# GpSimd splits each attention weight block in four pieces of 256 columns

## The chip, the cores and the metric

The kernel runs as one program on one core of a Trainium2 chip. The time is the device time of one execution in microseconds (us). Engine names in the rows: PE is TensorE (PEld its weight loads), DVE is VectorE, ACT is ScalarE, POOL is GpSimd, SP issues the DMAs of this kernel's weights.

## The reference

Two post-norm decoder layers over 1024 tokens (16 sequences of 64) of width 512, in fp32. Only the two grouped attentions matter here: layer 0's cross-attention (called B in the kernel, with rotary tables) and layer 1's self-attention (called D, with a sliding window). Each has 32 query heads and 8 key heads of 128:

```python
# B: _L0_xattn_ref (D is the same without cos/sin, with its own mask)
q = (query @ Wq).reshape(nb, q_len, H, D).transpose(0, 2, 1, 3)
k = (key @ Wk)...; v = (value @ Wv)...
q = q * cos + _rotate_half(q) * sin
k = k * cos + _rotate_half(k) * sin
scores = jnp.einsum('bhqd,bhkd->bhqk', q, k) / jnp.sqrt(jnp.float32(D))
attn = jax.nn.softmax(scores, axis=-1)
x = jnp.einsum('bhqk,bhkd->bhqd', attn, v)
return x @ Wo
...
x = _layernorm(x + _L0_xattn_ref(x, ctx_4096, ...), axis=-1)
```

## The kernel before

fp32 products are made of reduced-precision ones. Each operand is held as a high part (the value rounded to fp32r) and a low part (what is left), and a product is three matmuls: high by high, high by low, low by high (`three`). So each weight must be split before TensorE can use it. GpSimd does this in `grouped_attention`: a block of 128 partitions by 1024 columns (`BLK`) arrives by DMA in one of two buffers `raw`; `high_part` (L78) adds zero to it and writes the high part as fp32r; after a wait on `w_high`, L694 subtracts the high part from the raw block and writes the low part, which raises `w_low`.

An attention runs over 4 pairs of key heads. `START` projects values, keys and the first queries; then three loop passes (`TURN`, in a hardware loop) and one last pass (`LAST`) follow. A pass has 16 units u (`SLOTS`): two key heads (u = 0 to 7 and 8 to 15) by 8 token tiles. GpSimd splits 4 blocks in `START` (v, k, q0, q1), 10 per loop pass (o0, o1, q0, q1, k, v, o2, o3, q2, q3) and 6 in `LAST`: 40 blocks per attention, 80 in both. The o blocks are the output weights `wo`, the q blocks the query weights `wq`. A block's split may begin when TensorE has stopped using the old contents: o0 and o2 wait for `wo_used` (the first half of the last output product of a head), o1 and o3 for `y_done` of that tile, q0 to q3 for the query projection that used them last. GpSimd takes the blocks strictly in that order.

What TensorE does in the units that matter, in its own order:

- u = 7 or 15: output product of the head's last tile (L83, bankY from `wo` and `oT`), in whose middle `wo_used` is raised.
- u = 0 or 8: transposes of the softmax (L791, wait for `prob`, DVE's L950), scores of a later unit (L764), probabilities by values (L803), a query projection (L83, bankA from `xT` and `wq`).
- u = 1 or 9: transposes, scores, L803, then output(u - 1), which waits for o1 or o3 (`w_low`), then a query projection.
- u = 2 or 10: transposes, output(u - 1), L803, then scores of unit u + 2, which in B wait for the rotated queries of the last projection (`qk_done`, DVE's L925), then further projections.

DVE does per unit L932 (mask, reads PSUM), L936 (maximum), L939 (subtract), L944 (sum), L947 (reciprocal), L950 (multiply), L978 (low part of the head's output, reads PSUM) and L955 (residual, reads PSUM). In B it also rotates the queries: L919 (reads PSUM), L921 and L925. L939, L950, L921 and L925 are `tensor_tensor` with both inputs in SBUF.

The lines that the change touches:

```python
high_part(dst[name][0], raw[n % 2][:]).then_inc(w_high, 1)
pool.wait_ge(w_high, part.weights + n + 1)
nc.gpsimd.tensor_tensor(dst[name][1], raw[n % 2][:], f32(dst[name][0]), ALU.subtract).then_inc(w_low, 1)
```

Of the kernel before, what the change touches and what calls it, by code (L numbers as in the profile page):

```python
# [11 lines left out]
ALU = mybir.AluOpType  # L12
# [21 lines left out]
BLK = 1024  # L34
# [4 lines left out]
def f32(ap):  # L39
    return ap.bitcast(F32)  # L40


def build_program(nc, io):
# [3 lines left out]
    def sb(stack, name, shape, dt=F32):  # L47
        return stack.enter_context(nc.sbuf_tensor("sb_" + name, shape, dt))

    def sem(name):  # L50
        return ctx.enter_context(nc.semaphore(name))
# [6 lines left out]
    raw = [sb(ctx, f"raw{i}", [P, BLK]) for i in range(NRAW)]  # L58
# [17 lines left out]
    def high_part(dst, src):  # L76

        return nc.gpsimd.tensor_tensor(dst, src, zero[0:src.shape[0]].to_broadcast([src.shape[0], src.shape[1]]), ALU.add)  # L78
# [126 lines left out]
    w_high = sem("A_whigh"); w_low = sem("A_wlow"); zeroed = sem("A_zeroed")  # L205
# [361 lines left out]
    only_qk = lambda order: [x for x in order if x[0] in "QK"]  # L567
    TURN_BANKS, TURN_QK = len(TURN), len(only_qk(TURN))

    START_BLOCKS = ["v", "k", "q0", "q1"]  # L570
    TURN_BLOCKS = ["o0", "o1", "q0", "q1", "k", "v", "o2", "o3", "q2", "q3"]
    LAST_BLOCKS = ["o0", "o1", "q0", "q1", "o2", "o3"]

    class Part:

        def __init__(self, it, order, blocks):
# [3 lines left out]
            if started:  # L580
                self.banks, self.qks, self.weights = self.banks + len(START), self.qks + len(only_qk(START)), self.weights + len(START_BLOCKS)

# [21 lines left out]

    assert not any(len(x) % 2 for x in (START, TURN, LAST, START_BLOCKS, TURN_BLOCKS, LAST_BLOCKS))
    group_names = ("w_high", "w_low", "padded", "a_ready", "swapped", "roped", "turned", "qk_done", "v_done",
# [4 lines left out]
    def grouped_attention(tag, norm, first, source, rope, following):  # L611
# [6 lines left out]
        with ExitStack() as mem:  # L618
# [25 lines left out]
            dst = {"k": [w[:].rearrange("p h k n -> p (h k n)") for w in wk], "v": [w[:].rearrange("p k n -> p (k n)") for w in wv]}  # L644
# [4 lines left out]
            def run(engine, start, turn):  # L649

                start(Part(first, START, START_BLOCKS))
                with engine.Fori(first, final) as it:
                    turn(Part(it, TURN, TURN_BLOCKS))
                turn(Part(final, LAST, LAST_BLOCKS))

            with nc.Block() as block:
                @block.sync
                def _(sp):
                    if rope:
                        sp.dma_start(mask[:], io["mask"]).then_inc(in_bound, 16)  # L660
                    else:
                        sp.dma_start(bound[:], io["causal"]).then_inc(in_bound, 16)

                    def load(part):
                        for n in range(len(part.blocks)):
                            at = part.weights + n
                            if part.order is START and n < NRAW:
                                continue
                            sp.wait_ge(w_low, at - 1)
                            src = io["w_attn"][at] if part.order is not TURN else io["w_attn"][bass.ds(at, 1)].rearrange("a p c -> p (a c)")  # L670
                            sp.dma_start(raw[n % 2][:], src).then_inc(w_raw[n % 2], 16)
                    run(sp, load, load)
                    load_ahead(sp, w_low, (first + NPAIR) * len(TURN_BLOCKS), *following)

                @block.gpsimd
                def _(pool):
                    def split(part):
                        for n, name in enumerate(part.blocks):
                            if part.order is not START:
                                if name == "o0":  # L680
                                    pool.wait_ge(wo_used, part.it * 2 + 1)
                                elif name == "o1":
                                    pool.wait_ge(y_done, part.it * SLOTS + 2)
                                elif name == "o2":
                                    pool.wait_ge(wo_used, part.it * 2 + 2)
                                elif name == "o3":
                                    pool.wait_ge(y_done, part.it * SLOTS + NT + 2)
                                else:
                                    used = {"q0": ("Q", 5), "q1": ("Q", 7), "k": ("Q", 5), "v": ("Q", 5), "q2": ("Q", 13), "q3": ("Q", 15)}[name]
                                    pool.wait_ge(a_ready, part.bank(used) + 1)  # L690
                            pool.wait_ge(w_raw[n % 2], (part.weights + n - n % 2) * 8 + 16)
                            high_part(dst[name][0], raw[n % 2][:]).then_inc(w_high, 1)
                            pool.wait_ge(w_high, part.weights + n + 1)
                            nc.gpsimd.tensor_tensor(dst[name][1], raw[n % 2][:], f32(dst[name][0]), ALU.subtract).then_inc(w_low, 1)  # L694
                            if part.order is START and name == "k":
                                nc.gpsimd.memset(kt[:], 0.0).then_inc(padded, 1)
                    run(pool, split, split)
# [835 lines left out]
```

## Time and profile before

| | us |
|---|---|
| three runs | 1838.74, 1838.44, 1837.08 |
| median | 1838.44 |
| span of the profiled execution | 1832.8 |
| median less that span | 5.6 |
| PE busy | 1679.7 |
| DVE busy | 1065.0 |
| ACT busy | 603.0 |
| POOL busy | 525.5 |
| DMA of one raw block, from issue to landing (median of 80) | 3.5 |

The profiled execution's own time is its span of 1832.8 us from the first to the last instruction and what lies around it, for which 5.6 us is taken, the distance to the median. Attention B lies at about 260 to 938 us of the span, D at about 991 to 1583 us. In the timeline rows below an instruction has its start, its duration, its engine, line and operation, what it writes and reads, a count, and in brackets how long its engine had stood idle and who ended that. An instruction's duration includes time in which it was already issued and could not proceed.

### The profile page before, as it was taken

What the parts mean: (1) busy time and instruction counts of PE and PEld (TensorE: products, weight loads), DVE (VectorE), ACT (ScalarE), POOL (GpSimd) and SP (SyncE); (2) the same over time, 40 slices, a digit from 0 to 9 for tenths busy, and PEclk for the clock granted to TensorE, in tenths of its full rate; (3) what the DMA queues carried; (4) which work ended last, traced back from release to release, by engine and by line L of the source; (5) the groups of instructions that cost most, each with busy time, mean ns of one, the idle gap of its engine ahead of it and who ended that gap; (6) DMA issues with size and microseconds to landing.
All of it is one profiled execution on the core that took longest, in us unless ns stands there. A gap on an engine that the chain in (4) does not pass through costs nothing. (4 is left out here: it accounts for less than half of the span.)

```text
span 1832.8 us, 24019 instructions
## 1 busy us (share of the span) xinstructions
PE 1679.7 (92%) x8910; PEld 1336.7 (73%) x8910; DVE 1065.0 (58%) x2105; ACT 603.0 (33%) x1199; POOL 525.5 (29%) x297
## 2 busy tenths in 40 slices
PE   8897879889998988989888999999999999888998
PEld 6665658667776866777677777777877877676866
DVE  3878775766676577566754245355265245517645
ACT  2564533223322323232243222222222222425541
POOL 4316123330323052120133323233053031432330
PEclk9998999899998989999999999999999999999999
DMA  4002011110111020000010111011021010112231
GB/s 178 14 18 81 25 35 46 47 35 12 36 35 46 1 70 24 23 24 24 23 42 27 57 35 47 12 57 46 0 69 46 0 46 24 47 33 61 71 91 46
DMA packets 26173, 75.78 MB, mean 41 GB/s; under 512 B 3904, under 2 KB 4640, under 8 KB 25824
## 3 DMA queue, kind: packets, MB, share of 16 engines
q1 hardware_dynamic: 25696, 73.42, 12.4%
q8 instruction: 66, 1.08, 0.2%
q0 software_dynamic: 384, 1.05, 0.2%
q14 instruction: 27, 0.22, 0.0%
HBM read 72.36 MB, written 2.10 MB: 41 GB/s over the span
## 5 line engine op out<-in xcount | busy, mean ns | idle before, releaser
L83 PE MATMUL bankA<-sb_xT,sb_Bwq 128*128 128x512 f32 x768 | 196.7, 407 | 0.0
L83 PE MATMUL bankY<-sb_Bwo,sb_BoT 128*128 128x512 f32 x768 | 195.9, 405 | 0.2 <-DVE sb_BoT L978 0.2
L83 PE MATMUL bankY<-sb_Dwo,sb_DoT 128*128 128x512 f32 x768 | 192.3, 399 | 2.0 <-POOL sb_Dwo L694 1.8
L83 PE MATMUL bankA<-sb_xT,sb_Dwq 128*128 128x512 f32 x768 | 189.9, 396 | 0.0
L83 PEld LDWEIGHTS bankY<-sb_Bwo,sb_BoT 128*128 128x128 f32 x768 | 142.8, 192 | 44.2 <-issue 15.0
L83 PEld LDWEIGHTS bankA<-sb_xT,sb_Bwq 128*128 128x128 f32 x768 | 147.4, 195 | 36.0 <-issue 2.7
L83 PEld LDWEIGHTS bankY<-sb_Dwo,sb_DoT 128*128 128x128 f32 x768 | 139.8, 188 | 44.0 <-issue 10.9
L83 PEld LDWEIGHTS bankA<-sb_xT,sb_Dwq 128*128 128x128 f32 x768 | 142.3, 188 | 33.9 <-issue 2.7
L919 DVE TENSOR_TENSOR sb_BqT<-bankA,sb_Btable 128x512 f32<-128x512 f32 x64 | 44.3, 692 | 183.5 <-ACT sb_Bsw L842 183.5
L78 POOL TENSOR_TENSOR sb_Bwo<-sb_raw,sb_zero 128x1024 fp32r<-128x1024 f32 x16 | 31.3, 1955 | 372.9 <-PE bankY L83 364.3
L78 POOL TENSOR_TENSOR sb_Dwo<-sb_raw,sb_zero 128x1024 fp32r<-128x1024 f32 x16 | 31.6, 1973 | 335.1 <-PE bankY L83 335.1
L932 DVE TENSOR_TENSOR sb_Dsc<-bankA,sb_Dbound 128x256 f32<-128x256 f32 x64 | 27.0, 422 | 158.6 <-PE bankA L764 158.6
L955 DVE TENSOR_TENSOR sb_xtok<-sb_xtok,bankY 128x512 f32<-128x512 f32 x128 | 87.1, 680 | 51.8 <-PE bankY L83 51.7
L842 ACT ACTIVATE sb_Bsw<-bankA 64x512 f32<-64x512 f32 x160 | 94.8, 593 | 54.8 <-PE bankA L83 51.7
L978 DVE TENSOR_TENSOR sb_DoT<-bankO,sb_DoT 128x512 fp32r<-128x512 f32 x64 | 43.7, 683 | 109.4 <-ACT sb_DoT L880 109.4
L764 PE MATMUL bankA<-sb_Bkt,sb_BqT 128*128 128x128 f32 x512 | 77.8, 300 | 27.7 <-DVE sb_BqT L925 24.1
L764 PEld LDWEIGHTS bankA<-sb_Bkt,sb_BqT 128*128 128x128 f32 x512 | 69.7, 211 | 34.5 <-DVE sb_BqT L925 23.3
L921 DVE TENSOR_TENSOR sb_Bsw<-sb_Bsw,sb_Btable 128x512 f32<-128x512 f32 x80 | 85.3, 1066 | 0.0
L874 ACT ACTIVATE sb_Dpt<-bankT 128x256 f32<-128x256 f32 x64 | 24.6, 384 | 184.4 <-PE bankT L791 184.4
L336 PE MATMUL bankA<-sb_Akt,sb_Aqm 128*128 128x128 f32 x512 | 71.9, 286 | 5.8 <-ACT sb_Aqm L416 4.2
L874 ACT ACTIVATE sb_Bpt<-bankT 128x256 f32<-128x256 f32 x64 | 24.6, 384 | 157.6 <-PE bankT L791 157.5
L854 ACT ACTIVATE sb_Bsc<-sb_Bsc 128x256 f32<-128x256 f32 x64 | 26.6, 416 | 138.8 <-DVE sb_Bsc L939 138.8
(253 smaller groups left out, 3406.3 us busy)
## 6 DMA issues: line engine op xcount, KB each, us to landing
sb_raw<-in_w_attn SPq DMA_DIRECT2D x80, 512.0 KB, 3.5
sb_raw<-in_q_gu SPq DMA_DIRECT2D x22, 256.0 KB, 2.7
sb_raw<-in_q_d SPq DMA_DIRECT2D x11, 256.0 KB, 2.6
sb_rawx<-in_xT SPq DMA_DIRECT2D x4, 512.0 KB, 8.0
sb_raw<-in_wqk SPq DMA_DIRECT2D x8, 256.0 KB, 2.6
sb_xtok<-in_x_tok SPq DMA_DIRECT2D x1, 2048.0 KB, 12.7
sb_raw<-in_ctxT SPq DMA_DIRECT2D x4, 512.0 KB, 3.8
sb_raw<-in_ctx_tok SPq DMA_DIRECT2D x4, 512.0 KB, 3.8
```

The source lines that it names most:

```text
L78: return nc.gpsimd.tensor_tensor(dst, src, zero[0:src.shape[0]].to_broadcast([src.shape[0], src.shape[1]]), ALU.add)
L83: last = nc.tensor.matmul(out, lhs, rhs, start=start and i == 0, stop=stop and i == len(pairs) - 1)
L336: done = nc.tensor.matmul(bankA[n % 2][:, j * P:(j + 1) * P], qm[quad % 2][:, j, 2 * m:2 * m + 2, :].rearrange("p e q -> p (e q)"), window ...
L764: done = nc.tensor.matmul(bank[:, at:at + P], qT[:, 2 * t + b, 2 * hp:2 * hp + 2, :].rearrange("p h q -> p (h q)"), window(kt, 2 * t + b, ...
L842: nc.scalar.activation(sw[part.swap(x)][64 * i:64 * i + 64, :], bankA[part.buffer(x)][64 - 64 * i:P - 64 * i, :], ACT.Copy).then_inc(swapp ...
L854: nc.scalar.activation(flat, flat, ACT.Exp, scale=HD ** -0.5).then_inc(st["exp"], 1)
L874: nc.scalar.activation(pt[u % 2][:], bankT[u % 2][:, 0:GROUP * S], ACT.Copy).then_inc(pt_done, 1)
L919: nc.vector.tensor_tensor(to, bankA[part.buffer(x)][:].rearrange("p (b s) -> p b s", s=S), table[:, 0, half].rearrange("p (b s) -> p b s", ...
L921: nc.vector.tensor_tensor(b[:], b[:], table[:, 1, half], ALU.mult).then_inc(turned, 1)
L932: nc.vector.tensor_tensor(s3, bankA[part.buffer(("S", u))][:].rearrange("p (a c) -> p a c", a=2)[:, :, S:S + P], bound_of(u).unsqueeze(1). ...
L955: nc.vector.tensor_tensor(xtok[:, t, :], xtok[:, t, :], bankY[u % 2][:], ALU.add).then_inc(y_done, 1)
L978: nc.vector.tensor_tensor(oT[u % 2][1][:].rearrange("p h b q -> p b h q"), bankO[:, :, 0:GROUP * S].rearrange("p b (h q) -> p b h q", h=GR ...
```

## The change

Each block is split in four pieces of 256 columns: the high part of a piece, a wait for it, its low part, then the next piece. `w_high` now counts pieces; `w_low` still counts blocks and is raised by the low part of the last piece. All 80 blocks of the two grouped attentions are cut; the splits of the other stages are not.

```diff
+    PIECES = 4
...
-                            high_part(dst[name][0], raw[n % 2][:]).then_inc(w_high, 1)
-                            pool.wait_ge(w_high, part.weights + n + 1)
-                            nc.gpsimd.tensor_tensor(dst[name][1], raw[n % 2][:], f32(dst[name][0]), ALU.subtract).then_inc(w_low, 1)
+                            for i in range(PIECES):
+                                piece = slice(i * BLK // PIECES, (i + 1) * BLK // PIECES)
+                                high_part(dst[name][0][:, piece], raw[n % 2][:, piece]).then_inc(w_high, 1)
+                                pool.wait_ge(w_high, (part.weights + n) * PIECES + i + 1)
+                                low = nc.gpsimd.tensor_tensor(dst[name][1][:, piece], raw[n % 2][:, piece], f32(dst[name][0][:, piece]), ALU.subtract)
+                                if i == PIECES - 1:
+                                    low.then_inc(w_low, 1)
```

GpSimd's queue at the head of the loop body of attention B, before, with the semaphores that each row waits for (blocks o0 and o1; D's loop is the same with sb_Dwo; the register operations compute the values of the waits):

```order
L691 ISA [waits G_wo_used]
L78 TENSOR_TENSOR sb_Bwo0<-sb_raw0,sb_zero 128x1024 [waits G_raw0]
L693 REGISTER_ALU
L694 TENSOR_TENSOR sb_Bwo1<-sb_raw0,sb_Bwo0 128x1024 [waits G_w_high]
L683 ISA
L78 TENSOR_TENSOR sb_Bwo0<-sb_raw1,sb_zero 128x1024 [waits G_raw1,G_y_done]
L693 REGISTER_ALU
L694 TENSOR_TENSOR sb_Bwo1<-sb_raw1,sb_Bwo0 128x1024 [waits G_w_high]
```

The same place in the changed kernel, up to the end of block o0 and the first piece of o1:

```order
L78 TENSOR_TENSOR sb_Bwo0<-sb_raw0,sb_zero 128x256
L696 REGISTER_ALU
L697 TENSOR_TENSOR sb_Bwo1<-sb_raw0,sb_Bwo0 128x256 [waits G_w_high]
L78 TENSOR_TENSOR sb_Bwo0<-sb_raw0,sb_zero 128x256
L696 REGISTER_ALU
L697 TENSOR_TENSOR sb_Bwo1<-sb_raw0,sb_Bwo0 128x256 [waits G_w_high]
L684 ISA
L78 TENSOR_TENSOR sb_Bwo0<-sb_raw1,sb_zero 128x256 [waits G_raw1,G_y_done]
L696 ISA
L697 TENSOR_TENSOR sb_Bwo1<-sb_raw1,sb_Bwo0 128x256 [waits G_w_high]
```

No instruction moved against another: a pair of instructions became four pairs, a low part is followed by the next high part with no wait between them inside a block, and the queues of the other engines are the same.

## Rows read from the trace of the kernel before

**Rows 1.** The page: the span, and each engine's busy time
```profile
span 1832.8 us, 24019 instructions
PE 1679.7 (92%) x8910; PEld 1336.7 (73%) x8910; DVE 1065.0 (58%) x2105; ACT 603.0 (33%) x1199; POOL 525.5 (29%) x297
```

**Rows 2.** PE's waits: who waited for whom, us in total, times, longest
```profile
PE bankT L791 <- DVE sb_Bsc L950: 28.0, 9, 4.7
PE bankA L764 <- DVE sb_BqT L925: 24.1, 13, 3.7
...
PE bankT L791 <- DVE sb_Dsc L950: 6.0, 8, 0.8
...
PE bankY L83 <- POOL sb_Dwo L694: 1.8, 7, 0.3
```

**Rows 3.** POOL's groups of instructions: 256-column splits elsewhere, busy us, mean ns
```profile
L1004 POOL TENSOR_TENSOR sb_Fagu<-sb_raw,sb_Fagu 128x256 fp32r<-128x256 f32 x1 | 0.7, 724 | 0.1
L78 POOL TENSOR_TENSOR sb_Fagu<-sb_raw,sb_zero 128x256 fp32r<-128x256 f32 x1 | 0.6, 613 | 46.1 <-POOLq L1161 46.1
```

**Rows 4.** Timeline of attention D, a head's change, POOL, DVE and PE
```profile
1097.76 1.89 POOL L78 TENSOR_TENSOR sb_Dwo<-sb_raw,sb_zero 128x1024 fp32r<-128x1024 f32 x1 [33.31 <-PE bankY L83]
...
1100.63 3.04 PE L83 MATMUL bankA<-sb_xT,sb_Dwq 128*128 128x512 f32 x12
...
1102.08 2.07 POOL L78 TENSOR_TENSOR sb_Dwo<-sb_raw,sb_zero 128x1024 fp32r<-128x1024 f32 x1
...
1102.32 2.11 DVE L950 TENSOR_TENSOR sb_Dsc<-sb_Dsc,sb_Dri 128x256 f32<-128x256 f32 x1
...
1104.23 2.42 POOL L694 TENSOR_TENSOR sb_Dwo<-sb_raw,sb_Dwo 128x1024 fp32r<-128x1024 f32 x1
...
1104.49 0.44 PE L791 MATMUL bankT<-sb_ident,sb_Dsc 128*128 128x128 f32 x2 [0.81 <-DVE sb_Dsc L950]
...
1106.70 3.03 PE L83 MATMUL bankY<-sb_Dwo,sb_DoT 128*128 128x512 f32 x12 [0.25 <-POOL sb_Dwo L694]
```

**Rows 5.** Timeline of attention B, a head's change, POOL, DVE and PE
```profile
391.70 1.89 POOL L78 TENSOR_TENSOR sb_Bwo<-sb_raw,sb_zero 128x1024 fp32r<-128x1024 f32 x1 [39.30 <-PE bankY L83]
392.11 2.03 DVE L921 TENSOR_TENSOR sb_Bsw<-sb_Bsw,sb_Btable 128x512 f32<-128x512 f32 x1
...
393.67 2.71 POOL L694 TENSOR_TENSOR sb_Bwo<-sb_raw,sb_Bwo 128x1024 fp32r<-128x1024 f32 x1
...
394.24 2.69 DVE L925 TENSOR_TENSOR sb_BqT<-sb_BqT,sb_Bsw 128x512 f32<-128x512 f32 x1
...
394.58 3.04 PE L83 MATMUL bankA<-sb_xT,sb_Bwq 128*128 128x512 f32 x12
...
399.71 2.56 DVE L950 TENSOR_TENSOR sb_Bsc<-sb_Bsc,sb_Bri 128x256 f32<-128x256 f32 x1
...
402.32 0.69 PE L791 MATMUL bankT<-sb_ident,sb_Bsc 128*128 128x128 f32 x2 [4.70 <-DVE sb_Bsc L950]
...
405.61 3.01 PE L83 MATMUL bankY<-sb_Bwo,sb_BoT 128*128 128x512 f32 x12
```

**Rows 6.** Timeline of attention B, units 2 and 10: rotated queries and scores
```profile
413.93 2.45 DVE L921 TENSOR_TENSOR sb_Bsw<-sb_Bsw,sb_Btable 128x512 f32<-128x512 f32 x1
...
417.36 1.16 PE L764 MATMUL bankA<-sb_Bkt,sb_BqT 128*128 128x128 f32 x8 [2.34 <-DVE sb_BqT L925]
...
508.34 2.08 PE L764 MATMUL bankA<-sb_Bkt,sb_BqT 128*128 128x128 f32 x8 [3.60 <-DVE sb_BqT L925]
```

**Rows 7.** PE behind another wait, and stretches of B and D: busy us, then granted clock
```profile
890.51 0.69 PE L791 MATMUL bankT<-sb_ident,sb_Bsc 128*128 128x128 f32 x2 [4.61 <-DVE sb_Bsc L950]
...
894.00 4.34 PE L83 MATMUL bankY<-sb_Bwo,sb_BoT 128*128 128x512 f32 x12
...
294.00:938.00 644.00, 581.25 (x2897) 462.98 (x2896) 438.51 (x775) 197.78 (x375) 151.04 (x68) 0.95 0.09 29
991.00:1583.00 592.00, 578.56 (x3040) 465.35 (x3040) 268.48 (x543) 152.43 (x308) 175.48 (x81) 1.00 0.11 36
```

## The prediction

> **What bounds the kernel now.** I read the page first: TensorE is busy for 92% of the span and GpSimd for 29% [rows 1], so GpSimd's own time counts only where TensorE waits for it, directly or through VectorE. The view of TensorE's waits shows both. In B it waits 28.0 us for L950 and 24.1 us for L925; in D only 6.0 us for L950, and 1.8 us for GpSimd's low parts of wo, 7 times [rows 2]. Then the timelines show why. In B, L921, L925, L939 and L950, which read both inputs from SBUF, take 2.03, 2.69 and 2.56 us where 0.68 and 0.42 us are their undisturbed times; they end 0.3 to 0.55 us after the GpSimd instruction that ran when they were issued: L950, issued at 399.71, ends at 402.27 [rows 5]. So a 2 us GpSimd instruction holds VectorE, and TensorE stands for 4.70 us behind it. GpSimd is held in turn, but for less: the L694 behind L921 takes 2.71 us instead of 2.40, the L78 behind L939 in D 2.07 us instead of 1.89 [rows 4, 5].
>
> In D the second limit is visible. GpSimd begins o0 at 1097.76, ends o1 at 1106.65, and the output product starts at 1106.70 having waited 0.25 us for it [rows 4]. There is no slack there, at 7 places.
>
> **What a block costs.** A high and a low part of 256 columns exist elsewhere: 613 and 724 ns [rows 3]. With the 0.08 us between a high part and its low part (1097.76 + 1.89 to the next start) and the 0.03 us by which the next high part overlaps, a piece is 0.61 + 0.08 + 0.73 - 0.03 = 1.39 us, a block 5.56 us. Now it is 1.89 + 0.08 + 2.40 - 0.03 = 4.34 us. Each of 80 blocks grows by 1.22 us, 98 us of GpSimd time. 0.1 us either way per piece is my bound on this. For all blocks but o0 to o3 that growth is hidden: q, k and v blocks are used several units later, and the v block of D's start, needed soonest, ends just where TensorE finishes its transposes (0 to 0.1 us if that cover is gone). A DMA of a raw block waits for the block before last and lands in some 3.5 us, less than the 5.56 us of the block between.
>
> **D: seven heads' changes (slower).** New o0 and o1: 2 x 5.56 = 11.1 us, and four collisions with L939 and L950, at 0.04 to 0.18 us (the 2.07 against 1.89 is the largest [rows 4]), 0.4 us: GpSimd ends at 1097.76 + 11.6 = 1109.35. TensorE no longer waits 0.81 us for L950 and stands ready at about 1105.5, so it waits 3.9 us, and the output product starts 1109.40 - 1106.70 = 2.70 us later. 7 x 2.70 = 18.9 us. Nothing gives that back: VectorE and ScalarE wait for TensorE here.
>
> The Trainium skill (SBUF — State Buffer, Who interferes with whom) says that the loser of the port that GpSimd and VectorE share "fully blocks" for the whole instruction. Whole durations of 0.42 us for each of the four VectorE instructions would make the collisions 1.7 us and the sum 1.3 us more at each of the seven places; the rows show at most 0.18 us, so this case's trace does not bear out that price for GpSimd.
>
> **The clock.** D has a granted clock of 1.00 over its whole stretch, which is 2.4 GHz; B has 0.95, so about a tenth of B's time is at 1.2 GHz [rows 7]. In B each of the eight waits of 3.6 us or more is followed by such a time. Its price: from the transposes to the end of the output product, D needs 4.99 us without its wait [rows 4], B after its long waits 6.30 us at the least (402.32 to 408.62 [rows 5]) and 7.83 at the most (890.51 to 898.34 [rows 7]). The five places have a mean of 7.0, so 2.0 us each, bounds 1.3 and 2.8. D's new waits are of that length, so I take 7 x 2.0 = 14.0 us. Below stands 0: no D wait of before is long enough to show it. D's short wait of 0.48 us for L950 near its start goes: -0.4. D: 18.9 + 14.0 - 0.4 = +32.5 us.
>
> **B: heads' changes (about nothing).** Five of the seven look like rows 5, with waits of 4.6 to 4.7 us. With pieces, L921 and L925 each wait for at most one piece; L950 then ends at about 397.0, before TensorE ends its projection at 397.62. The 4.70 us are gone. What is late next is o1. GpSimd needs 11.1 us and meets eight colliding instructions, four of 512 columns at 0.31 to 0.45 us and four of 256 at 0.04 to 0.18: 1.9 us. It ends at 391.70 + 13.0 = 404.7, where the output product started at 405.61: 0.8 us earlier. TensorE stands 5.4 us ahead of it, so the 2.0 us of the slow clock now lie behind the start, where 0.6 us of them lay before (the product takes 3.01 to 4.34 us [rows 5, 7], mean 3.6, against 3.03). Net -0.8 + 2.0 - 0.6 = +0.6, five times +3 us. The other two changes, behind the loop's branch, had their output product 12.5 us after GpSimd's start; the same steps give 12.3: 0.
>
> **B: scores after the rotation (faster).** At 413.93 L921 waits for a whole high and low part (2.45 us), and the scores wait 2.34 us for L925 [rows 6]. GpSimd starts q1 at the end of the same projection, 2.43 us before L921 is issued. With pieces L921 ends 1.0 us after its issue (the piece that runs, then 0.55), L925, issued 0.3 us later, 0.7 us after that, and the scores start 1.4 us earlier than at 417.36, four places, -5.6. At three places L925 is held by the k block too (3.6 to 3.7 us [rows 6]); these end at the same 0.9 us: 3 x 2.75 = -8.3. One wait of the same kind at B's first units, within the 28.0 us of [rows 2], -1.7. The slow clock behind the three long ones (scores take 2.08 us instead of 1.16 [rows 6]) goes at 2.0 us each, behind two of the others at 1.5: -9.0, bounds 3 and 12. Sum -24.6, with the heads' changes -21.6 us.
>
> **Sum.** +32.5 - 21.6 = +10.9 us. On the profiled execution: span 1832.8 to 1843.7, and with the 5.6 us around it 1849.3, against the median of 1838.4. About 0.2%, 3.7 us, is what a measurement of this kernel can tell from no change.
>
> **Rivals.**
> *The clock stays high in D* (or VectorE's head start hides it). For it: D has lost no clock so far, its GpSimd waits were short. Against: B's long waits, all eight. 10.9 - 14.0 = -3: 1835 us.
> *Pieces cost less than their single rows*, because dispatch overlaps in a row of them; at 1.25 us a piece, o0 and o1 take 10.0 + 0.5 us: D +1.6 and +1.5 clock each, 22; B's five heads' changes 1.1 us earlier each, -2.5 in all; -24.6 stays, and the shorter waits save some 8 of clock in B. About -13: 1825 us. Against: the 0.03 us overlap is all that the rows show.
> *GpSimd is held for whole VectorE instructions*, which decides if VectorE wins every boundary: at D 1.3 us more each (9), at B's five 2 us (10), 20 in all: 1869 us. Against: the 2.07 and 2.71 us.
> *The change does not do what it says*: inside a block no wait separates a low part from the next high part, so VectorE might not get in there. Then B keeps its waits and GpSimd only grows: +32 in D, +5 in B: 1875 us. Against: the L78 of 1102.08 was issued before its predecessor's end and still yielded 0.18 us [rows 4].
>
> **How the numbers follow.** Forecast 0.60, its own range 1841 to 1858 (clock terms 1.3 to 2.8, pieces 0.05 either way); clock stays high 0.15; cheaper pieces 0.12; GpSimd held 0.08; no effect on VectorE 0.05. The range 1830 to 1866 leaves out the cheap pieces and half of the last two. Slower: 0.55 of the forecast and 0.13, 0.68. Same: 0.05 of the forecast and 0.10 of the clock case, 0.15. Faster: 0.12 and 0.05, 0.17.
>
> **What would show it.** L939, L950, L921 and L925 at most near 1.3 us; the 28.0 us for L950 in B nearly gone, L925 near 9 us; waits of PE for the low part of wo of about 3.9 us seven times in D and 5 us five times in B; D's granted clock down to about 0.97, B's near 0.96. Wrong if D's waits for GpSimd are under 2 us, if D's clock stays at 1.00, or if VectorE's instructions still take 2 us.

## The result, and the profile after

| | before | after |
|---|---|---|
| median, us | 1837.81 (1837.08 to 1838.74, 4 runs) | 1850.76 (1849.32 to 1854.07, 4 runs) |
| span of the profiled execution | 1832.8 | 1847.5 |
| attention B, from its first transposes to C's | 676.7 | 652.6 |
| attention D, the same way | 592.4 | 627.9 |
| all the rest of the span | 563.7 | 567.0 |
| POOL busy | 525.5 | 629.4 |
| DVE busy | 1065.0 | 965.4 |

The changed kernel is slower by 0.7%: ratio 1.007, 95% interval 1.0056 to 1.0084. A fourth run of before moved its median from the 1838.44 of the prediction to 1837.81. The forecast of 1849.3 us is 1.5 us below the measured median, the direction is right, and both attentions moved as forecast: B gained 24 us (forecast 21.6), D lost 35.5 us (forecast 32.5).

In the changed kernel the lines that concern us have moved: L694 is L697, L764 is L769, L791 is L796, L921 is L926, L925 is L930, L939 is L944 and L950 is L955. The page of after, which answers to [rows 1]:

```profile
span 1847.5 us, 24679 instructions
PE 1684.7 (91%) x8910; PEld 1342.2 (73%) x8910; DVE 965.4 (52%) x2105; ACT 602.3 (33%) x1199; POOL 629.4 (34%) x777
```

GpSimd has 480 instructions more and is busy 104 us longer; VectorE has the same 2105 instructions and is busy 100 us less, because it no longer stands issued behind GpSimd. TensorE's waits (total us, times, longest), which answer to [rows 2]:

```profile
PE bankY L83 <- POOL sb_Dwo L697: 29.7, 7, 4.4
PE bankY L83 <- POOL sb_Bwo L697: 28.2, 7, 5.7
...
PE bankA L769 <- DVE sb_BqT L930: 10.0, 13, 1.0
...
PE bankT L796 <- DVE sb_Bsc L955: 1.5, 2, 1.1
```

The wait for L955 in B fell from 28.0 to 1.5 us, the one for the rotated queries from 24.1 to 10.0 us. In their place stand waits for GpSimd itself: 28.2 us in B, where there were none in the list, and 29.7 us in D, where there were 1.8. One more wait fell, which neither the rows nor the prediction name: at B's start TensorE waits for VectorE to copy out the rotary tables. The wait in before and in after, then the two mask instructions that VectorE had to finish ahead of the copies in before, and the first of them in after:

```profile
PE bankO L710 <- DVE sb_Btable L907: 7.6, 1, 7.6
PE bankO L715 <- DVE sb_Btable L912: 3.5, 1, 3.5
```
```profile
268.86 3.86 DVE L903 TENSOR_SCALAR sb_Bhidden<-sb_Bmask 128x1024 f32<-128x1024 int32 x1
...
272.64 2.37 DVE L904 TENSOR_SCALAR sb_Bbound<-sb_Bmask 128x1024 f32<-128x1024 int32 x1
```
```profile
271.28 0.85 DVE L908 TENSOR_SCALAR sb_Bhidden<-sb_Bmask 128x1024 f32<-128x1024 int32 x1
```

So it is not only the `tensor_tensor` instructions with two inputs in SBUF that GpSimd's whole blocks held: these read one. The wait is 4.1 us shorter, a sixth of B's gain. Three of the seven groups of rotation and softmax instructions that GpSimd holds, each with its least, middle and greatest duration in ns (the greatest of the other four are 0.93 to 1.23 us):

```profile
L955 DVE TENSOR_TENSOR sb_Bsc<-sb_Bsc,sb_Bri x64: 416/420/969, 319.5 to 899.7; 128x256 f32<-128x256 f32 x64
L955 DVE TENSOR_TENSOR sb_Dsc<-sb_Dsc,sb_Dri x64: 416/424/968, 1016.8 to 1581.0; 128x256 f32<-128x256 f32 x64
L930 DVE TENSOR_TENSOR sb_BqT<-sb_BqT,sb_Bsw x64: 676/682/1255, 305.1 to 881.4; 128x512 f32<-128x512 f32 x64
```

None is above 1.3 us any more; in [rows 4, 5] they took 2.03 to 2.69. This is what the change does, and what each half of it costs is seen at a head's change. D, on POOL, DVE and PE, from the same timeline view as [rows 4]:

```profile
1079.65 1.02 POOL L697 TENSOR_TENSOR sb_Dwo<-sb_raw,sb_Dwo 128x256 fp32r<-128x256 f32 x1
...
1080.00 0.96 DVE L955 TENSOR_TENSOR sb_Dsc<-sb_Dsc,sb_Dri 128x256 f32<-128x256 f32 x1
...
1081.95 0.38 PE L796 MATMUL bankT<-sb_ident,sb_Dsc 128*128 128x128 f32 x2
...
1087.24 0.95 POOL L697 TENSOR_TENSOR sb_Dwo<-sb_raw,sb_Dwo 128x256 fp32r<-128x256 f32 x1
...
1088.25 5.23 PE L83 MATMUL bankY<-sb_Dwo,sb_DoT 128*128 128x512 f32 x12 [4.39 <-POOL sb_Dwo L697]
```

GpSimd began o0 at 1076.21. VectorE's L955 now takes 0.96 us, the transposes wait for nothing, and TensorE then stands 4.39 us before the output product, because the last low part of o1 ends at 1088.19. From GpSimd's start to the product are 12.04 us; in [rows 4] it was 8.94. And the product behind the wait takes 5.23 us instead of 3.03. B, the same view as [rows 5]:

```profile
383.41 1.05 POOL L697 TENSOR_TENSOR sb_Bwo<-sb_raw,sb_Bwo 128x256 fp32r<-128x256 f32 x1
...
387.07 0.96 DVE L955 TENSOR_TENSOR sb_Bsc<-sb_Bsc,sb_Bri 128x256 f32<-128x256 f32 x1
388.16 0.38 PE L796 MATMUL bankT<-sb_ident,sb_Bsc 128*128 128x128 f32 x2
...
394.91 0.79 POOL L697 TENSOR_TENSOR sb_Bwo<-sb_raw,sb_Bwo 128x256 fp32r<-128x256 f32 x1
395.76 5.04 PE L83 MATMUL bankY<-sb_Bwo,sb_BoT 128*128 128x512 f32 x12 [5.69 <-POOL sb_Bwo L697]
...
408.11 1.16 PE L769 MATMUL bankA<-sb_Bkt,sb_BqT 128*128 128x128 f32 x8 [0.91 <-DVE sb_BqT L930]
```

Here the 4.70 us wait of [rows 5] is gone from the transposes and a wait of 5.69 us stands before the product. The scores of unit 2 (last row) wait 0.91 us where they waited 2.34 [rows 6]. The stretches of B and D (busy us of PE, PEld, DVE, ACT and POOL with their instructions, then the granted clock, the DMA share and GB/s):

```profile
264.20:916.80 652.60, 597.18 (x3056) 478.89 (x3056) 395.10 (x794) 205.00 (x388) 241.27 (x321) 0.96 0.11 34
970.40:1598.30 627.90, 592.03 (x3041) 476.54 (x3042) 231.17 (x543) 152.44 (x308) 218.10 (x322) 0.96 0.11 34
```

D's granted clock went from 1.00 [rows 7] to 0.96, which is time at 1.2 GHz that D had hardly any of before; B's rose from 0.95 to 0.96.

### The profile page after: what moved, and what is told of

The parts are those of the page before. It is cut to its first block and busy times, and to the rows that moved or that the text cites. A ratio compares the mean times of both kernels' runs of the same rounds, so it can differ in the third digit from the quotient of the medians.

```text
span 1847.5 us, 24679 instructions
## 1 busy us (share of the span) xinstructions
PE 1684.7 (91%) x8910; PEld 1342.2 (73%) x8910; DVE 965.4 (52%) x2105; ACT 602.3 (33%) x1199; POOL 629.4 (34%) x777
## 5 line engine op out<-in xcount | busy, mean ns | idle before, releaser
L83 PE MATMUL bankY<-sb_Dwo,sb_DoT 128*128 128x512 f32 x768 | 207.4, 422 | 30.0 <-POOL sb_Dwo L697 29.7
L83 PE MATMUL bankY<-sb_Bwo,sb_BoT 128*128 128x512 f32 x768 | 203.7, 417 | 28.4 <-POOL sb_Bwo L697 28.2
L83 PEld LDWEIGHTS bankY<-sb_Dwo,sb_DoT 128*128 128x128 f32 x768 | 150.6, 202 | 75.8 <-POOL sb_Dwo L697 32.5
L83 PEld LDWEIGHTS bankY<-sb_Bwo,sb_BoT 128*128 128x128 f32 x768 | 148.5, 199 | 73.2 <-POOL sb_Bwo L697 31.0
L78 POOL TENSOR_TENSOR sb_Bwo<-sb_raw,sb_zero 128x256 fp32r<-128x256 f32 x64 | 46.2, 722 | 317.5 <-PE bankY L83 317.5
L78 POOL TENSOR_TENSOR sb_Dwo<-sb_raw,sb_zero 128x256 fp32r<-128x256 f32 x64 | 41.7, 651 | 319.7 <-PE bankY L83 319.7
L769 PE MATMUL bankA<-sb_Bkt,sb_BqT 128*128 128x128 f32 x512 | 69.8, 279 | 14.6 <-DVE sb_BqT L930 10.0
L769 PEld LDWEIGHTS bankA<-sb_Bkt,sb_BqT 128*128 128x128 f32 x512 | 62.2, 191 | 21.4 <-DVE sb_BqT L930 10.6
L336 PEld LDWEIGHTS bankA<-sb_Akt,sb_Aqm 128*128 128x128 f32 x512 | 64.4, 198 | 8.7 <-ACT sb_Aqm L416 6.4
L769 PE MATMUL bankA<-sb_Dkt,sb_DqT 128*128 128x128 f32 x512 | 69.0, 278 | 0.0
```

What stands on the lines that cost most here:

```text
L83: last = nc.tensor.matmul(out, lhs, rhs, start=start and i == 0, stop=stop and i == len(pairs) - 1)
L336: done = nc.tensor.matmul(bankA[n % 2][:, j * P:(j + 1) * P], qm[quad % 2][:, j, 2 * m:2 * m + 2, :].rearrange("p e q -> p (e q)"), window ...
L769: done = nc.tensor.matmul(bank[:, at:at + P], qT[:, 2 * t + b, 2 * hp:2 * hp + 2, :].rearrange("p h q -> p (h q)"), window(kt, 2 * t + b, ...
```

## The experiments

**The theory.** Cutting a block does two separate things. VectorE is held by GpSimd for one piece instead of a whole block, which shortens TensorE's waits for VectorE. And each block takes GpSimd 1.2 us longer, which delays what waits for the whole block: the output product behind o0 and o1, or o2 and o3. The first pays in B, at the scores; the second costs in D, and costs once more because TensorE runs at 1.2 GHz behind the new waits. **The rivals:** the pieces themselves (their interleaving with VectorE, their waits) cause D's loss, not their length; the heads' changes of B carry the gain; VectorE gets in only because of the waits between a high part and its low part.

All versions compute the whole reference. In the diffs `many` is the number of pieces of a block and takes the place of `PIECES`; the values of the waits on `w_high` (`highs_before`, the pieces split so far) follow it. In the kernels of the experiments the lines are numbered again: L711, L713 and L715 are the low part (L694 before), L783 the scores, L810, L812 and L814 the transposes, L944 to L948 the last step of the rotation, L969 to L973 L950.

| kernel | median, us | ratio to before | B, us | D, us | rest |
|---|---|---|---|---|---|
| before | 1839.1 | | 676.7 | 592.4 | 563.7 |
| after | 1850.76 | 1.007 | 652.6 | 627.9 | 567.0 |
| e1: four pieces in B alone | 1819.43 | 0.9897 | 653.6 | 593.6 | 567.2 |
| e2: four pieces in D alone | 1876.03 | 1.0198 | 677.7 | 629.3 | 568.0 |
| e3: q, k, v in four, o whole | 1815.90 | 0.9874 | 653.4 | 593.4 | 567.7 |
| e4: two pieces | 1817.44 | 0.9891 | 640.1 | 604.7 | 567.7 |
| e5: whole blocks, D's o0 and o2 one high part longer | 1861.46 | 1.0127 | 676.8 | 615.4 | 566.3 |
| e6: four pieces, wait in mid-product | 1826.90 | 0.9942 | 641.9 | 616.2 | 566.5 |
| e7: four highs, then four lows | 1839.44 | 1.0007 | 656.3 | 621.2 | 568.5 |
| e8: two pieces in B, wait in mid-product | 1792.73 | 0.9745 | 632.8 | 591.4 | 567.9 |
| e9: B q, k, v in four, o in two; D whole; wait in mid-product | 1782.34 | 0.9690 | 623.6 | 590.5 | 568.8 |

B, D and rest are of each kernel's one profiled execution. The median of before is of the runs beside the first four kernels (1837.8 to 1839.2 beside the others); 0.001 of a ratio is 1.8 us.

### Four pieces in one attention alone

```diff
-                            for i in range(PIECES):
+                            many = 4 if tag == 'B' else 1    # e2: 4 if tag == 'D' else 1
+                            for i in range(many):
```

> Pieces of 256 columns in attention B alone, whole blocks in D. Theory (B gains because VectorE is let in between pieces, D loses because o0 and o1 take GpSimd 3 us longer): B's stage 24 us shorter as in the changed kernel, D's as before, 592 us and clock 1.00; median about 1814. Rival (the loss is not D's own, for instance the clock of the whole program): D's stage is longer than 596 us here too, median over 1820.

> Pieces in attention D alone, whole blocks in B. Theory: B's stage as before (677 us), D's stage 628 us as in the changed kernel, median about 1873. Rival (D's loss was partly brought in from B): D's stage under 615 us, median under 1860.

Measured 1819.43 (ratio 0.9897, 0.988 to 0.9913) and 1876.03 (1.0198, 1.0181 to 1.0215). TensorE's waits with pieces in B alone, then in D alone:

```profile
PE bankY L83 <- POOL sb_Bwo L711: 27.5, 7, 5.4
...
PE bankA L783 <- DVE sb_BqT L944: 10.3, 13, 1.1
...
PE bankT L810 <- DVE sb_Dsc L969: 6.1, 8, 0.8
...
PE bankY L83 <- POOL sb_Dwo L711: 1.8, 7, 0.3
```
```profile
PE bankT L810 <- DVE sb_Bsc L969: 27.2, 9, 4.7
...
PE bankY L83 <- POOL sb_Dwo L711: 30.2, 7, 4.4
```

Each half carries its own rows and leaves the other attention with its rows of before. By stage lengths the halves are -23.1 us in B and +36.9 us in D, 13.8 us together where the whole change has 11.4; by medians -19.7 and +36.9, 17.2 against 13.0. So they add, to within 4 us. The change is a gain of about 20 us and a loss of about 37 us, and no coupling shows beyond those 4 us.

### Where in B the gain is

```diff
+                            many = 1 if name[0] == 'o' else 4
```

> Pieces for the blocks of q, k and v in both attentions; the eight o blocks of each pass whole. Theory: D as before (no q, k or v block is waited for), the 4.7 us waits of B's transposes stay, the seven waits of B's scores for the rotated queries fall from 2.3 to 3.7 us to 0.9 us, and with the clock behind them this is 20 to 25 us: median about 1815. Rival (B's gain came with the waits of the transposes, and the waits of the scores move elsewhere): within 5 us of the kernel before, about 1835.

Measured 1815.90 (0.9874, 0.9857 to 0.989). TensorE's waits:

```profile
PE bankT L810 <- DVE sb_Bsc L969: 26.7, 9, 4.7
PE bankA L783 <- DVE sb_BqT L944: 10.3, 13, 1.0
```

The long waits at B's heads' changes have stayed, because the o blocks are whole, and B is as short as with all blocks cut: 653.4 us against 653.6. The whole gain of B comes with the q, k and v blocks, and cutting o0 to o3 there exchanges 26.7 us of waits for VectorE against 27.5 us of waits for GpSimd (e1). The rival that B's heads' changes carry the gain falls. Most of the gain is at the scores, but not all: the wait for the rotary tables is down to 3.6 us here too. The kernel was profiled once more, to see how well stage lengths repeat (its label says b_only, it is the kernel of e3):

> The version with only the q, k and v blocks in pieces, looked at once more for what its stages take in a second profiled execution: theory: B's stage within 2 us of 653 us, D's within 2 us of 593 us; rival (the stages' times depend on where the slow clock happens to fall by more than that): 5 us or more apart.

One run of 1813.78 us, B 652.1 and D 593.3 against 653.4 and 593.4. The stage lengths of this kernel repeat within 1.4 us, and B's whole blocks take 676.7, 677.7 and 676.8 us in before, e2 and e5, so differences between stages from some 3 us on can be read.

### Two pieces instead of four

```diff
+                            many = 2
```

> Two pieces of 512 columns for all blocks. Theory, from the rows of 512 columns (1.04 and 1.29 us): a block takes 4.76 us; the output product in D starts 1.0 us later seven times, behind waits of 2.2 us, and half of these are followed by a slow clock, +14 us; in B the output products start 2.6 us earlier before clock (-6 us after it) and the scores gain a little less, -21 us: median about 1825. Rival (what costs in D is the mere number of instructions that VectorE can hold, not the length of the two blocks): D's loss is half of the changed kernel's, +17 us, and B as there: 1831.

Measured 1817.44 (0.9891, 0.987 to 0.9911), 7.6 us less than expected. TensorE's waits:

```profile
PE bankA L783 <- DVE sb_BqT L944: 18.1, 13, 2.3
PE bankY L83 <- POOL sb_Dwo L711: 14.8, 7, 2.4
PE bankY L83 <- POOL sb_Bwo L711: 7.8, 6, 1.5
```

D behaves as expected: from GpSimd's start to the product 9.94 us in the mean, 1.0 more than before, and D is 12.3 us longer (14 expected). B gained 36.6 us and not 27. Against e1 its waits for GpSimd are 19.7 us less (7.8, none above 1.5), those at the scores 7.8 us more, those for L969 5.0 us more and the one for the rotary tables 1.1 us more: 5.8 us less in all. B is 13.5 us shorter, so some 7.7 us more lie elsewhere; the slow clock behind the long waits can carry them, for B's granted clock is 0.98 here and 0.96 in e1, and all seven output products behind a head's change take 3.01 to 3.06 us, where five took 5.03 to 5.49 us. This is what I had left out. Where all blocks are cut alike, two pieces are better than four: the smallest piece is not the best.

### Is it GpSimd's length, or the pieces?

Whole blocks everywhere, and in D the high part of o0 and of o2 is written twice, which changes no value and makes GpSimd 2 us later.

```diff
+                            many = 1
+                            if tag == "D" and name in ("o0", "o2"):
+                                high_part(dst[name][0], raw[n % 2][:]).then_inc(w_high, 1)
+                                pool.wait_ge(w_high, highs_before(tag, part, n) + 1)
```

> Whole blocks everywhere as in the kernel before; in D alone the high part of o0 and of o2 is written twice, which adds 1.9 us to GpSimd and no pieces. Theory (D loses what o0 and o1 take longer, plus the clock behind the wait): the output product starts 1.9 us later seven times behind waits of about 2.1 us, the clock costs 0.7 us each: D's stage 592 + 18 = 610 us, median about 1857. Rival (D's loss comes from the pieces themselves, the many instructions and their collisions): D's stage within 3 us of 592, median under 1842.

Measured 1861.46 (1.0127, 1.011 to 1.0144). TensorE's waits and one product behind them:

```profile
PE bankY L83 <- POOL sb_Dwo L715: 15.4, 7, 2.2
```
```profile
1111.07 4.51 PE L83 MATMUL bankY<-sb_Dwo,sb_DoT 128*128 128x512 f32 x12 [2.21 <-POOL sb_Dwo L715]
```

No block is cut, and D is 23.0 us longer: the product starts 1.97 us later at seven places, 13.8 us, and the other 9 us are products and projections at the slow clock, as in the row, 4.51 us instead of 3.03; five of the seven products are like it, two take 3.02 and 3.03. This is the loss of D without the pieces. The rival that pieces as such cause it falls, and the absence of slack that the prediction read from one row, 0.25 us of wait at the product [rows 4], is confirmed: each us on GpSimd there is a us of D, and the slow clock behind the new waits comes on top. That clock cost more than expected here, 1.3 us a place and not 0.7.

### Giving TensorE something to do in the wait

Output product of a head's first tile: the products with the first two heads of the group need only o0 (or o2), those with the last two o1 (or o3). The wait for the second block can stand between them.

```diff
                         if u % NT == 0:
-                            pe.wait_ge(w_low, part.block("o3" if u else "o1"))
+                            pe.wait_ge(w_low, part.block("o2" if u else "o0"))
...
+                        elif u % NT == 0:
+                            product(bankY[u % 2][:], pairs[:len(pairs) // 2], stop=False)
+                            pe.wait_ge(w_low, part.block("o3" if u else "o1"))
+                            product(bankY[u % 2][:], pairs[len(pairs) // 2:], start=False).then_inc(y_ready, 1)
```

> The changed kernel, and TensorE waits for block o0 (or o2) before the output product of a head's first tile and for o1 (or o3) only in the middle of that product, since its first six matmuls use o0 alone. Theory (the low part of o1 ends last): its second half still starts with the end of o1, so six matmuls, 1.45 us and up to 2.4 us at the slow clock, leave the path twelve times, D 10 to 17 us and B 7 to 12 us shorter: median about 1830. Rival (the wait is for what stands before o1, or the clock takes it back): within 5 us of the changed kernel, about 1848.

Measured 1826.90 (0.9942, 0.9924 to 0.996), 23.9 us below the changed kernel, which differs in this alone. TensorE's waits, and one product of D in its two halves:

```profile
PE bankY L83 <- POOL sb_Bwo L711: 19.6, 6, 3.8
PE bankY L83 <- POOL sb_Dwo L711: 19.2, 7, 2.8
```
```profile
1073.04 1.65 PE L83 MATMUL bankY<-sb_Dwo,sb_DoT 128*128 128x512 f32 x6
1077.53 2.93 PE L83 MATMUL bankY<-sb_Dwo,sb_DoT 128*128 128x512 f32 x6 [2.83 <-POOL sb_Dwo L711]
```

Half the product runs while GpSimd still works on the second block. Each wait is some 1.5 us shorter, the length of half a product: 7 of them in D make 10.5 us, and D is 11.7 us shorter. The slow clock is seen behind fewer waits: in the row the second half takes 2.93 us where the first took 1.65, but only three of D's seven second halves are that slow (2.48 to 2.93 us), the others take 1.65 to 1.88. D's granted clock is 0.97 where it was 0.96.

### The order of the high and low parts

Four high parts back to back, one wait, four low parts: the same instructions with one wait in place of four.

```diff
-                                pool.wait_ge(w_high, (part.weights + n) * PIECES + i + 1)
+                            pool.wait_ge(w_high, highs_before(tag, part, n) + many)
+                            for i in range(many):
+                                piece = slice(i * BLK // many, (i + 1) * BLK // many)
                                 low = nc.gpsimd.tensor_tensor(dst[name][1][:, piece], raw[n % 2][:, piece], f32(dst[name][0][:, piece]), ALU.subtract)
```

> Four pieces, but the four high parts of a block first and then its four low parts, one wait between. Theory: VectorE gets in at a boundary with no wait too, so its instructions stay at 1.3 us or less; three gaps of 0.08 to 0.11 us per block go, 0.6 us for o0 and o1 together: D 4 us and B 3 us shorter, median about 1843. Rival (VectorE gets in only where GpSimd waits for a semaphore): VectorE's instructions take 2 us and more again, B's waits of 4.7 us for L950 are back, median over 1860.

Measured 1839.44 (1.0007, 0.9995 to 1.002, 10 runs of 1836.91 to 1847.82), 11 us below the changed kernel. A step of the rotation that came while four low parts ran, GpSimd first (one row for the four), then VectorE:

```profile
394.38 3.73 POOL L713 TENSOR_TENSOR sb_Bwo<-sb_raw,sb_Bwo 128x256 fp32r<-128x256 f32 x4
```
```profile
395.44 1.23 DVE L946 TENSOR_TENSOR sb_BqT<-sb_BqT,sb_Bsw 128x512 f32<-128x512 f32 x1
```

VectorE is let in after one piece although no wait stands between the pieces, and no rotation or softmax instruction of this version is above 1.3 us. So for them the port changes hands at the end of each GpSimd instruction, also where the next one is ready: the rival that VectorE needs the waits falls, and with it what was left of "the change does not do what it says". What the three waits of a block cost shows in D: from GpSimd's start to the product 11.14 us against 11.9, and TensorE waits

```profile
PE bankY L83 <- POOL sb_Dwo L713: 24.3, 7, 3.5
```

24.3 us instead of 29.7. D is 6.6 us shorter. B reads 3.7 us longer, but this profiled execution was the longest of the ten, 8.4 us above the median; what B's share of the 11 us is stays open.

### A version that beats both

Taken together: no cut where there is no slack behind GpSimd and no wait for VectorE to win (D); in B the q, k and v blocks in pieces; the o blocks in few; and the wait in mid-product.

```diff
+                            many = 2 if tag == 'B' else 1                                  # e8
+                            many = 1 if tag == 'D' else 2 if name[0] == 'o' else 4         # e9
```

> Two pieces of 512 columns in B, whole blocks in D, and the wait for o1 in the middle of the product. Theory: B's stage as with two pieces everywhere (640 us) and 3 to 8 us less by the later wait, since 7.8 us of waits for GpSimd stand there; D as before or 2 to 6 us less: 592 to 586; median 1790 to 1800. Rival (the wait in the middle only moves the waiting to VectorE's results): 640 and 592, median 1802.

> As the version with two pieces in B, whole blocks in D and the wait for o1 in the middle of the product, but q, k and v blocks of B in four pieces, the o blocks of B in two. Theory (each block cut as its place asks: short holds of VectorE where the scores wait for the rotation, a short block where the output product waits): the scores' waits for the rotated queries fall from 14.5 us to the 10 us of the changed kernel, B's stage 4 us shorter than 633 us, D's 592 us: median about 1788. Rival (the longer q0 block makes q1 and the scores late again): no gain, 1793 or more.

Measured 1792.73 (0.9745, 0.9729 to 0.9761) and 1782.34 (0.969, 0.9677 to 0.9704, 5 runs). TensorE's waits in e8, then in e9:

```profile
PE bankA L783 <- DVE sb_BqT L948: 14.5, 13, 2.2
PE bankT L814 <- DVE sb_Bsc L973: 7.4, 12, 1.1
```
```profile
PE bankA L783 <- DVE sb_BqT L948: 9.0, 13, 0.9
PE bankT L814 <- DVE sb_Bsc L973: 7.0, 7, 1.1
PE bankT L814 <- DVE sb_Dsc L973: 6.1, 8, 0.8
```

No matmul of either attention waits for GpSimd's weights any more. A head's change of B in e9:

```profile
392.61 0.44 PE L814 MATMUL bankT<-sb_ident,sb_Bsc 128*128 128x128 f32 x2 [1.13 <-DVE sb_Bsc L973]
...
394.51 3.26 PE L83 MATMUL bankY<-sb_Bwo,sb_BoT 128*128 128x512 f32 x12
```

Where before waited 4.70 us and after 5.69, this one waits 1.13 us. The stretches of B and D in e9, read as above, show the clock at 0.99 in both:

```profile
262.00:880.00 618.00, 585.17 (x3039) 466.42 (x3038) 410.55 (x791) 202.26 (x384) 228.44 (x257) 0.99 0.12 36
943.00:1535.00 592.00, 579.91 (x3048) 467.39 (x3048) 277.31 (x543) 153.41 (x309) 176.39 (x82) 0.99 0.12 36
```

B is 53 us shorter than before, D 2 us. Against e8, B is 9.2 us shorter where 4 were expected: the scores' waits fell by 5.5 us, and the wait for the rotary tables, which the expectation did not name, from 6.7 to 3.4 us.

## Why the prediction was right, step by step

**D, the length of a block: right.** Forecast 5.56 us for a block without collisions. In the changed kernel two undisturbed pieces start 1.38 us apart (1076.21 and 1077.59), 5.5 us a block. GpSimd's busy time rose by 104 us (98 forecast, collisions not in it). The group of wo's low parts, busy us, then mean ns with the collisions in it, answers to [rows 3]:

```profile
L697 POOL TENSOR_TENSOR sb_Dwo<-sb_raw,sb_Dwo 128x256 fp32r<-128x256 f32 x64 | 49.8, 778 | 5.0
```

The rival of cheaper pieces falls: undisturbed pieces take 0.61 and 0.73 us, as in [rows 3].

**D, the start of the product: the mechanism right, one term too small.** Forecast 2.70 us later at each place. Measured, the starts lie 11.9 us behind GpSimd's in the mean, against 8.94: +3.0 us, 20.9 us in all instead of 18.9. The term that was mis-sized is the price of a collision for GpSimd. I took 0.04 to 0.18 us from whole blocks. The low part beside L955 at 1079.65 took 1.02 us instead of 0.73, the one at 1087.24 took 0.95. Five of the sixteen instructions of o0 and o1 are longer than undisturbed at each place, by 0.05 to 0.29 us, 0.7 to 0.9 us together, where I had four and 0.4 us. So the waits are 4.24 us in the mean and not 3.9.

On this price the Trainium skill (SBUF — State Buffer, Who interferes with whom) says that the one that issues second "fully blocks". For VectorE's rotation and softmax instructions the trace agrees: they take up to 2.8 us behind a whole block, up to 1.26 behind a piece, which is about the rest of GpSimd's instruction and their own work. For GpSimd it agrees in part only: its pieces lost 0.05 to 0.58 us to instructions that take 0.42 and 0.68 us undisturbed, more than I had put it at in D, and at none of the places read a whole one. The rival that GpSimd is held for whole instructions (1869 us) falls with that.

**D, the clock: right.** Forecast 14.0 us. The seven products behind the waits take 4.37 to 5.49 us instead of 3.03, 13.4 us in all. D's granted clock is 0.96 (0.97 forecast), so some 7 to 8% of D's time was at 1.2 GHz, of which the 1.00 of [rows 7] shows nothing. The rival "the clock stays high" falls. 20.9 + 13.4 - 0.4 is 33.9 of the measured 35.5 us.

**B, the scores: the waits right, the sum partly by luck.** Forecast -24.6 us: 13.9 for the seven waits, 1.7 for one at B's first units, 9.0 for the clock. With the o blocks whole, so that only q, k and v change, B is 23.3 and 24.7 us shorter in two profiles. The seven waits are now 0.8 to 1.0 us, the forecast 0.9, and the scores' waits are 13.8 us less. But two terms were wrong. The wait for the rotary tables, 4.1 us of gain, is not in the sum at all: the prediction names only VectorE instructions with both inputs in SBUF as held, and the mask instructions L903 and L904, which read one, were held too. The one at the first units gave 0.8 us and not 1.7. What is left for the clock, when all changed waits of these two profiles are taken off, is about 6 us and not 9.0. The missing gain and the oversized terms roughly cancel.

**B, the heads' changes: right.** Forecast +3 us. The product was forecast 13.0 us behind GpSimd's start and a wait of 5.4 us before it; measured 13.04 to 13.16 us at the five places, and waits of 5.4 to 5.7. These products take 5.04 to 5.49 us, 5.18 in the mean, where they took 3.01 to 4.34, 3.60 in the mean. So the start comes 0.9 us earlier (0.8 forecast) and the product is 1.6 us longer (2.0 - 0.6 forecast), +0.7 for each of the five. The stage says the same. From GpSimd's first start on o0 behind a head's change to the end of B are 534.1 us in after and 535.2 in e1, where the o blocks are cut, and 531.9 and 532.3 in the two profiles of e3, where they are whole: 1.8 to 3.3 us more.

Yet B as a whole is as long with the o blocks cut (652.6 and 653.6 us) as without (653.4 and 652.1). The difference lies ahead of the first head's change, a stretch of 118.5 and 118.4 us against 121.5 and 119.7. GpSimd splits the first o0 and o1 of the loop there, and only where they are whole does TensorE wait for the rotated keys: 2.1 us in e3, 0.6 us in its second profile. The prediction has no term for this gain of 1 to 3 us.

**Outside the two attentions.** The rest of the span is 3.4 us longer in after, and I had forecast nothing. It is no effect of the change: it is 566 to 569 us in every other version too, e5 included, which touches D alone. Most of it lies ahead of B, 261.8 us in before and 264.1 to 266.5 in every other version. The profiled execution of before was the short one, which is also why its span lay 5.6 us under the median and that of after 3.3. The 5.6 us were not time around the span, as the prediction took them: in after the profiled execution's time is 1849.3 us for a span of 1847.5, so 1.8 us lie around it. The sum came out because the short execution was inside the 5.6.

**Sum.** Stage by stage -24.1 + 35.5 = +11.4 us against +10.9 forecast. The nearness of the two owes something to luck: B was 2.5 us better and D 3.0 us worse than their terms, and B's own sum holds the two errors that cancel.

## What to carry to other kernels

Where GpSimd and VectorE share a port, the length of GpSimd's instructions is a dial: a shorter one lets VectorE in sooner and makes the whole job longer, so cut only those jobs whose consumer has slack, and only as fine as the wait it removes. Look for each job at who waits for its end: here the q, k and v blocks had slack, and a wait of 0.25 us at the product showed that the o blocks had none. And look for held VectorE instructions by their durations, not by their kind: two that read a single SBUF input cost 4.1 us at B's start. A new wait of TensorE is charged again in clock: in this kernel waits of 4 us or more cost some 2 us more each, those around 2 us 0.8 to 1.3 us (e4, e5); putting the wait in the middle of the product that needs the block took 24 us off without any other change.

## What the runs showed of the hardware

- Two pieces back to back, without a wait between them, let VectorE in as readily as two with a wait (1.23 us for a 128x512 step in e7). For these `tensor_tensor` instructions it is the length of one GpSimd instruction that sets how long VectorE is held, not what stands behind it in the queue.
- A mask instruction of 128x1024 with one SBUF input did not get in at such a boundary: L903 took 3.86 us in before, issued during L694, and ended 0.5 us after the MEMSET that GpSimd ran next; in after the same instruction took 0.85 us. Why it stood through both, no run shows. The row reductions (L936 and L944), also with one SBUF input, took 0.40 to 0.42 us at all their places and were never held.
- The price of cutting on GpSimd is about 0.2 us an instruction: 0.61 and 0.73 us for 256 columns (after), 1.04 and 1.29 for 512 (e9), 1.89 and 2.40 for 1024 (before). Waits between a high part and its low part add 0.08 us each, and leaving out three of four saved 0.4 us a block in e7, where the collisions fall otherwise too.
- The slow clock was more frequent behind longer waits here, but the length alone did not decide it. Behind D's waits of 4.1 to 4.4 us in after all 7 products were slow, behind 2.2 us in e5 5 of 7, and of the five waits of 2.4 us in e4 four; behind its two of 1.5 us none. This row of e4 is one of the four:

```profile
1073.73 4.61 PE L83 MATMUL bankY<-sb_Dwo,sb_DoT 128*128 128x512 f32 x12 [2.37 <-POOL sb_Dwo L711]
```
